# Layer norms computed on token rows instead of through matrix products, with the output product by rows and a new order of work

## The reference, cut

```python
def _layernorm(x, axis=-1, eps=1e-05):
    m = jnp.mean(x, axis=axis, keepdims=True)
    v = jnp.var(x, axis=axis, keepdims=True)
    return (x - m) / jnp.sqrt(v + eps)
...
# tok: z, f, o = tanh, sigmoid, sigmoid of a convolution of width 2
c = ft * c + (1.0 - ft) * zt          # scan over the rows
return (c, ot * c)
...
# attn: 8 heads of 16; each row looks back by 39 offsets (0 to 32, 48, 64, 96, 128, 192, 256)
scores = jnp.einsum('bhnd,bhond->bhon', q, km) / math.sqrt(HD)
...
out = jnp.einsum('bhon,bhond->bhnd', attn, vg)
gate = jax.nn.sigmoid(x @ W_gate + b_gate)
return out_flat * gate @ W_out + b_out
...
# ffn: 64 experts share the weights w1, w2; top 2 of a softmax, 128 places per expert
h = jax.nn.gelu(jnp.einsum('nh,fh->nf', buf, w1) + b1, approximate=False)
y = jnp.einsum('nf,hf->nh', h, w2) + b2
...
h = _L0_tok_ref(x, ...)
h = h + _L0_attn_ref(_layernorm(h, axis=-1), ...)
h = h + _L0_ffn_ref(_layernorm(h, axis=-1), ...)
```

## Time and profile before

| | |
|---|---|
| median of 3 runs | 496.3 us (495.8 to 497.25) |
| profiled execution, its own time | 499.14 us |
| span of its trace | 497.3 us |
| PE busy | 473.4 us, 95% |
| DVE busy | 404.3 us, 81% |
| POOL busy | 396.5 us, 80% |
| ACT busy | 303.0 us, 61% |
| granted TensorE clock, mean | 0.991 |

### The profile page before, as it was taken

The page is one execution under the profiler, slowest core; times in us unless marked ns, Lnnn a source line. Parts: engine busy times, 40 slices in busy tenths (PEclk is TensorE's granted clock), DMA queues, the critical chain, the costliest instruction groups (busy, mean ns, idle before and its releaser), DMA issues.

```text
span 497.3 us, 12720 instructions
## 1 busy us (share of the span) xinstructions
PE 473.4 (95%) x4698; PEld 298.6 (60%) x4698; DVE 404.3 (81%) x837; ACT 303.0 (61%) x539; POOL 396.5 (80%) x444
## 2 busy tenths in 40 slices
PE   7689799999999999999999999999999999999994
PEld 5334446465665666666566556656655666658673
DVE  3678797888888898888789788888978889878764
ACT  4456566665765756566475657657555665747664
POOL 6299989997987879698878969878796988986511
PEclk9799999999999999999999999999999999999999
DMA  6000539080724417081542707145180633535901
GB/s 246 15 1 1 132 62 190 11 181 2 180 28 115 94 58 150 2 192 16 129 79 57 151 1 181 27 112 97 52 157 1 164 45 94 100 96 97 192 18 31
DMA packets 54222, 44.27 MB, mean 89 GB/s; under 512 B 27248, under 2 KB 41488, under 8 KB 54032
## 3 DMA queue, kind: packets, MB, share of 16 engines
q1 hardware_dynamic: 54160, 43.45, 39.5%
HBM read 24.59 MB, written 18.85 MB: 87 GB/s over the span
## 4 chain that ended last, share of the span: by engine, by line
PE 79%; DVE 6%; POOL 5%; issue 4%; DMA 4%; ACT 2%; SPq 1%; POOLq 0%; DVEq 0%; ACTq 0%
PE bank L367 19%; PE bank L353 8%; PE bank L462 7%; PE bank L485 6%; PE bank L332 6%; PE bank L333 5%; PE bank L430 4%; PE bank L417 3%; PE bank L341 2%; PE bank L346 2%; PE bank L409 2%; PE bank L381 2%; PE bank L437 2%; PE bank L442 2%; PE bank L447 2%
## 5 line engine op out<-in xcount | busy, mean ns | idle before, releaser
L1140 POOL TENSOR_TENSOR prod<-q,k 128x1496 f32<-128x1496 f32 x48 | 144.0, 3014 | 13.3 <-ACT q L630 13.3
L850 DVE SCALAR_TENSOR_TENSOR prod<-bank,par,k 128x1496 f32<-128x1496 f32 x80 | 139.5, 1768 | 7.5 <-ACT q L630 7.5
L1182 POOL TENSOR_TENSOR acc<-acc,tmp 128x310 f32<-128x310 f32 (+4 forms) x80 | 64.8, 810 | 38.4 <-DVE tmp L907 24.1
L367 PE MATMUL bank<-prod,ew 128*32 128x374 f32 x1024 | 90.3, 481 | 0.8 <-DVE mixin L817 0.8
L1125 POOL TENSOR_TENSOR fprod<-q,k 128x374 f32<-128x374 f32 (+6 forms) x112 | 80.2, 746 | 0.0
L654 ACT ACTIVATE scT<-bank 128x374 f32<-128x374 f32 x48 | 23.2, 484 | 64.8 <-PE bank L367 64.8
L353 PE MATMUL bank<-xn,par 128*128 128x374 f32 x128 | 53.7, 506 | 2.9 <-DVE xn L839 2.9
L485 PEld LDWEIGHTS bank<-par,hid 128*128 128x128 f32 x384 | 47.6, 191 | 9.9 <-issue 6.8
L367 PEld LDWEIGHTS bank<-prod,ew 128*32 128x32 f32 x1024 | 28.9, 110 | 37.6 <-issue 34.7
L485 PE MATMUL bank<-par,hid 128*128 128x128 f32 x384 | 50.1, 275 | 0.9 <-ACT hid L713 0.9
L907 DVE TENSOR_TENSOR tmp<-bank,vT 128x310 f32<-128x310 f32 (+4 forms) x80 | 30.3, 380 | 23.9 <-PE bank L409 22.2
(11 more groups left out here) (130 smaller groups left out, 977.4 us busy)
## 6 DMA issues: line engine op xcount, KB each, us to landing
band_scratch<-attn SPq DMA_DIRECT2D x16, 769.5 KB, 6.0
band<-band_scratch SPq DMA_DIRECT2D x64, 192.0 KB, 3.8
v<-v_scratch SPq DMA_DIRECT2D x32, 192.0 KB, 5.0
v_scratch<-vtok SPq DMA_DIRECT2D x16, 192.0 KB, 4.1
xT<-x_dram SPq DMA_DIRECT2D x16, 187.5 KB, 4.2
out_dram<-osb SPq DMA_DIRECT2D x16, 128.0 KB
par<-params_dram SPq DMA_DIRECT2D x1, 1819.5 KB, 7.7
out_dram<-osb SPq DMA_DIRECT2D x16, 59.0 KB
```

Source lines behind the costliest of these rows:

```text
L367: done = mm(home(f"s{c}")[32 * g:32 * g + 32, 0:N], ew[:, c * CW + j, :], src[:, j, :], start=first or only, stop=last or only)
L850: v.scalar_tensor_tensor(bass.AP(prod[c][:, :, :].tensor, part * N, [[CW * N, 128], [PARTS * N, w], [1, N]]), home("q")[:, 0:N].unsqueeze( ...
L1140: g.tensor_tensor(bass.AP(prod[c][:, :, :].tensor, part * N, [[CW * N, 128], [PARTS * N, w], [1, N]]), q[q_.s][:, :].unsqueeze(1).broadcas ...
L1182: g.tensor_tensor(acc[:, o:N], acc[:, o:N], tmp[i % 2][:, o:N], ALU.add).then_inc(acc_added[i], 1)
```

## The change

1. Norm 1: h is transposed to rows (`turn_h`, three 128x128 transpositions), DVE takes mean and variance of each row by `bn_stats` and `bn_aggr` (`stats1`), ACT takes ln and exp of 128x3 numbers, DVE makes a shift (`shift_rows`), ACT scales and shifts the rows with both as per-partition operands (`norm1_rows`), `turn_x` transposes back and ACT copies (`norm1_back`). `center`, `variance`, `norm_square` and `norm1` go. The kept h is written by ACT from the transposed h (`keep_rows`), and POOL adds the bias of W_out to it.
2. `out_project` gives rows (three products of 128x128, with ao as the stationary side), so h2 is in rows; norm 2 is done the same way, with one transposition (`turn_x2`), and `turn_h2` goes.
3. The far scores are transposed as a third group of their own (`turn_scores` 2, `score_add` 2) and line 384's small products go; the far offsets stand in another order, so that the second of their two sets of sums leaves out the first 96 columns.
4. All orders (PE, ACT, DVE, POOL, SP), lags and bank homes are written anew. ACT's turn has four table loads. SP writes and reads the band ahead of `load_x`.

```diff
-            def center(q_, *before):
+            def turn_h(q_, *before):
...
-                mm(home("hc")[:, 0:N], P("cen4"), h[q_.s][:, :], start=True, stop=True).then_inc(hc_mm, 1)
-
-            def variance(q_, *before):
-                freed(pe, before)
-                pe.wait_ge(sq_ready, q_.b + 1)
-                mm(home("var")[:, 0:N], P("avg"), stat[:, :], start=True, stop=True).then_inc(var_mm, 1)
+                for t in range(TT):
+                    done = tr(home("ht")[:, t * 128:(t + 1) * 128], h[q_.s][:, t * 128:(t + 1) * 128], ident)
+                done.then_inc(h_turned, 1)
+
+            def turn_x(q_, *before):
+                freed(pe, before)
+                pe.wait_ge(xrow_ready, q_.b + 1)
+                for t in range(TT):
+                    done = tr(home("xb")[:, t * 128:(t + 1) * 128], xrow[:, t, :], ident)
+                done.then_inc(x_turned, 1)
...
+                lo = SHORT if c == CH and not first else 0
...
             def out_project(q_, *before):
...
-                mm(home("op")[:, 0:N], P("outw"), ao[:, :], start=True, stop=True).then_inc(out_mm, 1)
...
+                for t in range(TT):
+                    done = mm(home("op")[:, t * D:(t + 1) * D], ao[:, t * 128:(t + 1) * 128], P("outw"), start=True, stop=True)
+                done.then_inc(out_mm, 1)
...
+            def norm1_rows(q_):
+                act.wait_ge(shift_ready, q_.b + 1)
+                after(act, x_turned, q_.b)
+                for t in range(TT):
+                    done = A(xrow[:, t, :], home("ht")[:, t * 128:(t + 1) * 128], ACT.Identity,
+                             bias=shift[:, t:t + 1], scale=rstd[:, t:t + 1])
+                done.then_inc(xrow_ready, 1)
...
+            def norm1_back(q_):
+                act.wait_ge(x_turned, q_.b + 1)
+                after(act, gate_mm, q_.b - 1)
+                A(xn[q_.s][:, :], home("xb")[:, 0:N], ACT.Copy, scale=-1.0).then_inc(xn_ready, 1)
...
+            def stats1(q_):
+                dve.wait_ge(h_turned, q_.b + 1)
+                for t in range(TT):
+                    done = v.bn_stats(part[:, t, :], home("ht")[:, t * 128:(t + 1) * 128])
+                done.then_inc(part_ready, 1)
+                dve.wait_ge(part_ready, q_.b + 1)
+                after(dve, rstd_ready, 2 * q_.b)
+                for t in range(TT):
+                    done = v.bn_aggr(stat[:, t, :], part[:, t, :])
+                done.then_inc(stat_ready, 1)
...
+                v.scalar_tensor_tensor(shift[:, :], stat[:, :, 0], -1.0, rstd[:, :], ALU.mult, ALU.mult)\
+                    .then_inc(shift_ready, 1)
...
+                if a3:
+                    write_attn(a3)
+                    read_band(a3)
                 if a0 and not (isinstance(a0.b, int) and a0.b < 2):
                     load_x(a0)
```

More of the change, by code:

```diff
@@ L18 @@
 NFAR = len(FAR)
[L19 removed]
+FAR_ORDER = [96, 48, 128, 64, 192, 256]
+OFFS = [LOCAL - j for j in range(DENSE)] + FAR_ORDER
 NO = len(OFFS)
@@ L502, in turn @@
+                if a1:
+                    turn_h(a1, ("fw", a3), ("ht", a2))
                 if a4:
-                    attend(a4, 2)
+                    turn_x2(a4, ("v", a2), ("op", a4))
+                if a3:
+                    spread_far(a3, 1, ("f", a1), ("bc5", a4), head=True)
+                    spread_far(a3, 0, ("s2", a2), ("pos", a5))
                 if a2:
-                    score(a2, 2, 0, ("tb0", a4), ("bc3", a4), ("bc0", a4), ("v", a3), ("up3", a6), ("s2", a3), first=True)
@@ new lines, in turn @@
+                if a4:
+                    attention_gate(a4)
+                if a3:
+                    softmax_gain(a3)
+                    softmax_out(a3)
+                if a5:
+                    keep(a5)
+                if a4:
+                    residual(a4)
+                if a5:
+                    take_room(a5)
+                if a2:
+                    products(a2, 0, 0)
+                if a4:
+                    stats2(a4)
+                if a1:
+                    recur_in(a1)
@@ L1017, in turn @@
+                if a2:
+                    products(a2, 0, 3)
+                if a4:
+                    shift2_rows(a4)
+                if a1:
+                    recur(a1)
+                if a5:
+                    weight_sum(a5)
+                if a1:
+                    recur_out(a1)
+                if a2:
+                    products(a2, 1, 0)
                 if a3:
                     far_value(a3, 1)
+                if a5:
+                    gate_sum(a5)
+                if a3:
+                    far_value(a3, 0)
@@ L1019, in turn @@
+                if a1:
+                    stats1(a1)
+                if a5:
+                    gate_weight(a5)
+                    add_b2(a5)
+                if a2:
+                    score_add(a2, 2)
+                if a5:
+                    finish(a5)
+                if a1:
+                    shift_rows(a1)
+                if a4:
+                    route_max(a4)
                 if a2:
                     score_add(a2, 0)
-                    score_max(a2)
-                if a3:
-                    far_value(a3, 2)
@@ L1076, in turn @@
                 if a3:
-                    residual(a3)
+                    far_value(a3, 2)
                 if a4:
                     route_hits(a4)
-                if a1:
-                    score_add(a1, 1)
-                if a4:
                     route_mask(a4)
+                if a3:
+                    far_value(a3, 3)
+                if a2:
+                    score_add(a2, 1)
+                if a3:
+                    far_value(a3, 4)
+                if a2:
+                    score_max(a2)
+                if a3:
+                    far_value(a3, 5)
             pipeline(dve, turn, 5)
```

636 lines of the change are left out of this document (296 added, 340 removed).

## The result

The changed kernel takes **528.98 us** (median of 4 runs, 528.53 to 530.18), the kernel before 496.77 beside it: 1.0637 times, 95% interval 1.0609 to 1.0664. I had forecast 470. The profiled execution has a span of 526.7 us. The medians further down leave out one execution each of e_ctrl2 and e_nonorm_old that ran in a slower state of the chip (513.04 and 502.74 us).

What follows compares the result with a forecast made beforehand. PE was taken as the bound, DVE close behind. Turn 29.1 to 27.2 us saves 30.4 over 16 sequences; 499.14 - 30.4 + 4 = 472.7, with the median 2.84 below the profiled run: 470 us, range 458 to 490.

Steps and rivals of the forecast that it cites:

- PE's arithmetic: PE's work in a steady turn: 4.19 us removed, 1.99 added, net -2.36, so 29.1 becomes 26.7 us.
- The 0.5 us that I added for handovers: Steady turn: DVE's waits reach PE, adding 0.5 us to PE's 26.7 for a turn of 27.2.
- my sum less the shifts: DVE's busy time in a turn, forecast to go from 24.66 to 26.4 us, without the 0.3 for two shifts.
- Four loads of 1.28 a turn: ACT's table loads: two more each turn, 2.6 us, within ACT's at most 22.9 us.
- Two shifts of 128x3 at line 998's 0.14, 0.3.: DVE's added work per turn: the shifts of both norms, priced at 0.14 us each, together 0.3.
- DVE's 25.4 to 27.2: Range of DVE's busy time in a turn, in us, around the forecast 26.4.
- My sign that I would be wrong: Signs named: DVE busy above 27.2 us a turn, DVE idle over 2 us, or start over 10 us longer.
- DVE is the bound and dear: Rival: `bn_stats` at its upper price and 1 us of handovers, turn of 28.2, 486 us; chance 0.20.
- DVE keeps its idle time: Rival: DVE still waits 4.9 us a turn in the new order, turn of 31.3, 535 us; chance 0.10.
- I add 4: Start: longer chain from h to xn costs +1 to +3.6 us in one or two turns, taken as 4.

Runs made afterwards that it cites:

- e_ctrl2: Kernel before plus two unused 128x3 DVE operations at two places beside GpSimd products, a reciprocal and one with two SBUF inputs; 508.09 us, ratio 1.0169.
- e_nonorm_old: Kernel before in its own order, norms and output product by rows, norm 2's shift on ACT, norm 1 left out (values not the reference's); 495.36 us.
- e_actshift: Changed kernel with the shifts of both norms made on ACT instead of DVE, right values kept; 496.78 us, ratio 0.9959 to the kernel before.
- e_one: Changed kernel with norm 2's two-input shift replaced by a reciprocal of one input (value wrong); 497.84 us.
- e_best2: e_setup with norm 1's rows made on DVE in one operation from PSUM and DVE's one-time setup moved behind the first sequence's rows; 491.17 us.
- e_setup: e_actshift with DVE's one-time setup moved behind the first sequence's statistics; 491.64 us.
- e_oldorder: Kernel before with its own order, lags and two table loads; only norms and output product by rows, both shifts on ACT; 511.92 us.

## Why the prediction was wrong

**Right: PE's arithmetic, and nearly ACT's and DVE's.** PE's turn without the lock is 26.77 us (e_actshift), forecast 26.7. The 0.5 us that I added for handovers does not show there. `bn_stats` took 278 ns where I had written 330, and `bn_aggr` 160 where I had 170 to 220. DVE without the shifts is busy 25.2 us a turn in e_actshift (201.7 in the last eight), where my sum less the shifts gives 26.1, so it was 0.9 too high. That e_one has DVE at 26.3 and a turn of 27.09, against 26.4 and 27.2 forecast, is luck: 1.25 us of its busy time are the lock on the shift of norm 1, 1.39 us there in a steady turn. Four loads of 1.28 a turn were there, and hidden in the steady state. ACT is busy 22.0 of the changed kernel's 28.8 (22.93 of 30), forecast at most 22.9.

**Wrong, first step: "Two shifts of 128x3 at line 998's 0.14, 0.3."** They took 2.36 + 0.43 us a turn on average (2.60 and 0.14 in the steady turns), and line 998's own operation went from 0.22 to 0.79 (0.74). Line 998 was the nearest row by shape, but its 0.22 was the price of a place where POOL's instructions are short (0.7 us each at 241.6). Both have two SBUF inputs, and such an operation costs what is left of POOL's running instruction, up to 3.3 us, wherever it lands. I gave that price no range at all, and DVE's 25.4 to 27.2 had room for `bn_stats` only. The 1273 ns of line 780 in the trace of before, which my prediction does not use, would have been a first row for it. With the steady prices the sum would have been 26.4 - 0.3 + 2.7 + 0.5 = 29.3 us; DVE was busy 28.0 in a turn of 28.8, lower mostly by the 0.9 us of the paragraph above. My sign that I would be wrong (DVE above 27.2 in a turn) came true. None of the rivals was this one: "DVE is the bound and dear" had the right engine and put the price on `bn_stats`; "DVE keeps its idle time" came nearest in time (535 us) by a mechanism that did not occur, since DVE idles 0.8 us in a turn.

**Wrong, second step: "I add 4"** for the start. I compared two chains of operations (3.5 us before, 4.5 and the loads after) and had "one or two turns" pay the difference. The outside grew by 34. Of it the experiments take off, one at a time from e_actshift: DVE's setup 5.1 us, which I had not looked for although the diff moved the statistics behind it; the two more loads 4.6; 0.9 us of each norm's chain 3.4 beyond the turn. In the old order, rows in place of products alone add up to 19 us outside (31.5 to 50.9; 16 if the profiled execution is put at the median), and leaving norm 1 out takes off up to 11. The new order with its two more loads has 15 more with norm 1 out on both sides, and the larger part of the loss is at the end, to which I had given nothing. These shares come from different kernels and are not a sum that closes. That the end turns wait for short chains with few sequences under way is read from the windows and was not tried by itself; whether another order could keep 26.8 us a turn and the old end stays open.

**Where the gain went.** PE's 2.3 us a turn were all there, 37 us over 16 turns. The lock took 16 x (28.8 - 26.77) = 32 of them, and the outside grew by 34: together a span 29 us longer.

## What to carry to other kernels

Before pricing a small DVE operation by its size, count its SBUF inputs and look at what GpSimd runs beside it: with two, or as a `tensor_scalar` from SBUF to SBUF, it may cost the whole of a GpSimd instruction, and the profile shows that as busy time of DVE. A reciprocal, ACT, or a place where GpSimd is idle avoids it. An operation that costs nothing today can begin to cost when something else moves it: e_best2's 2.77 us and norm 1's shift in e_one came about so.

A rewrite that moves work from a full engine to a longer chain gains in the steady turns and pays in the first and last ones; with 16 turns these were as much as the gain. Read both ends apart from the steady state: the distance from first to last output against so many full turns, and one run with half the sequences.

## What the runs showed that I had not expected

- A `tensor_scalar` of 128x3 from SBUF to SBUF took 159 to 3342 ns beside GpSimd's products, a reciprocal of the same size 165 to 169.
- What waits for the lock is decided by order: two locking operations in a row waited once, the second took 149 ns (median).
- PE's granted clock, 1.00 (2.4 GHz) in every steady window of e_setup, is a mean of 0.89 between its two levels (1.2 and 2.4 GHz) in the window at its end where PE idled for 6 us. So there an idle PE costs twice. It is not so everywhere: in e_oldorder from 453.5 to 483.5 us PE idles for 4.5 us and the clock is 1.00. The whole of e_setup has PE busy for 448.3 us where 473.4 less 16 x 2.3 would be 436.6. Two turns of the changed kernel took 30.2 us with the clock at 0.94. PE idles no more in them than in the others (1.9 us of 30.2, 2.0 of 28.8), and what lowered the clock there stays open. One of them in a window:

```profile
171.45:201.64 30.19, 28.34 (x300) 19.47 (x296) 28.18 (x63) 21.84 (x43) 24.45 (x27) 0.94 0.39 87
```
